# A top-k search on VectorE, with the last round of half the units read from a copy that GpSimd makes

## The chip, the cores and the metric

The kernel runs on one core of a Trainium2 chip. Its engines each work off their own queue in order: TensorE (PE in the profile, PEld for its weight loads), VectorE (DVE), ScalarE (ACT), GpSimd (POOL), and SyncE (SP), which only starts DMAs. They wait for each other through semaphores. The metric is the device time of one execution in microseconds (us); lower is better.

## The reference

Input x is 16 x 512 x 256 in float32. Three blocks follow one another, each added to x after a layernorm: half of an FFN, an attention, and half of the same FFN again.

```
x = x + 0.5 * ffn(layernorm(x))
x = x + attn(layernorm(x))
x = x + 0.5 * ffn(layernorm(x))
```

The attention has 16 heads of 16 columns and keeps, in each row of scores, only those at or above the 31st largest (U = int(5 * log(512)) = 31):

```
scores = einsum('bhqd,bhkd->bhqk', Q, K) / sqrt(D)
thresh = top_k(scores, U)[0][..., -1:]
scores = where(scores < thresh, -inf, scores)
attn = softmax(scores); context = attn @ V; out = context @ Wo.T + bo
```

The FFN routes each row over 16 experts (a gate with a fallback to the two best), mixes q, k and v of the experts by the weights, does causal attention over 512 rows, and mixes again through o_proj.

## The kernel before

The rows are cut into 64 tiles of 128. Three streams run together, each some tiles behind the one before: FFN job b (the first FFN), the attention, and FFN job a (the second). The order is written out by hand: a batch is a window of 64 slots (SPAN), and emit() walks the slots for each engine. The table AT and the constants above it (SC, EV, TOP, OUTS, GAP, TR, ...) say in which slot each step stands. An engine does the slots strictly in order, so a step at slot 7 waits behind everything that its engine has at slots up to 6. Batches 2 to 13 are a hardware loop (Fori), the others are written out.

A unit is one head of one tile: 128 rows by 512 scores. There are 1024; a slot is one unit, four units are a quad, two are a pair. For each quad:
- TensorE makes four score banks at slot 2 (L482), and ScalarE copies them into the ring S of 16 units at slot 3 (L709).
- VectorE searches two pairs, at slots 4 and 6 (TOP, L804 to L818). A search has 7 passes: MAX8 finds the 8 largest of each row and puts them into M8, MATCH_REPLACE writes a copy W in which these 8 are replaced by -3e38, and so on; 4 MAX8 and 3 MATCH_REPLACE. The two units of a pair alternate. The 31st largest is column TH = 30 of M8.
- ScalarE makes OUT = relu(threshold - S) at slot 7 (L720), which is above zero only where a score falls out, and the gap S = max - S at slot 9 (L724).
- TensorE transposes both into a bank, OUT times 2^80 (STEEP), at slot 16 (TR, L516 and L518); ScalarE takes exp (L715); TensorE multiplies by V (L542).

Between these stand the FFN's steps. On GpSimd they are HS (L913, hidden rows times gate weights, for which TensorE waits at L497), mixT (L931), the gate (L887 to L895) and many 1-wide ones for the norms, nmry (L942) among them. On VectorE they are small: v_a and v_b (L789), the replacement for the fallback (L793), a row maximum (L797) and a reciprocal (L784), at the end of a slot, behind a search. held() (L243) is a wait that also raises a counter of its engine. Some names share a buffer group in the profile: M is M8 (in the small jobs, mr is the pair to be replaced), L491 to L500 is the expert product.

Of the kernel before, what the change touches and what calls it, by code (L numbers as in the profile page):

```python
# [120 lines left out]

def build(nc, x, wqk, bqk, wv, bv, wo, bo, sim, gates, wf, wof, out):
    with ExitStack() as ctx:
# [225 lines left out]
        def _(pe):  # L349
# [151 lines left out]
            def slot(w, j):  # L501
# [6 lines left out]
                if at := due(w, j, TR, 4, QUADS * NB):  # L508
                    n, c = at
                    pe.wait_ge(s_ev, w.count(SPAN, 4 * (c + 4)) if w.lo != w.hi else min(4 * (n + 4), UNITS * NB))  # L510
                    for h in range(HG):
                        pe.wait_ge(s_gap, w.count(SPAN, 4 * c + h + 1))
                        r = (4 * c + h) % RING
                        for k in range(TPB):
# [3 lines left out]
                            mm = nc.tensor.matmul(pST[h][:, keys], OUT[:, r, keys], steep[:], start=False, stop=True)  # L518
# [234 lines left out]
        def _(dve):  # L753
# [46 lines left out]
            def slot(w, j):  # L800
# [3 lines left out]
                if at := due(w, j, TOP, 2, PAIRS * NB):  # L804
                    n, c = at
                    src = [S[:, (2 * c + i) % RING, :] for i in range(2)]
                    for k in range(PASSES):
                        for i in range(2):
                            m = M8[:, (2 * c + i) % RING, k // 2 * 8:k // 2 * 8 + 8]
                            if k == 0:  # L810
                                held(dve, s_ev, w.count(SPAN, 2 * c + i + 1))
                            else:
                                held(dve, s_tk, w.count(PAIRS * 2 * PASSES, c * 2 * PASSES + 2 * k + i - 1))
                            if k % 2 == 0:
                                nc.vector.max(m, src[i]).then_inc(s_tk, 1)  # L815
                            else:
                                nc.vector.match_replace(W[:, i, :], m, src[i], -BIG).then_inc(s_tk, 1)  # L817
# [174 lines left out]
```

## Time and profile before

| | |
|---|---|
| timed runs | 4924.1, 4924.43, 4927.03 us; median 4924.43 |
| the profiled execution | 4928.28 us, of which the span is 4925.7 |
| mean granted TensorE clock | 0.916 of full speed |
| busy: VectorE, TensorE, ScalarE, GpSimd | 4551.0, 4153.2, 3405.1, 2370.9 us |
| MAX8, 512 wide | 4096 of them, 0.68 us each |
| MATCH_REPLACE, 512 wide | 3072 of them, 0.68 us each |

Busy time is the time in which at least one instruction of an engine was running; two that overlap count once, so the mean duration of an instruction is longer than its share of the busy time. In a timeline, rows of the same line that follow each other are merged (x2 is two instructions, and the time is that of both). "[1.47 <-DVE M L815]" is idle time ahead of the row and what ended it.

### The profile page before, as it was taken

To read this page: it belongs to the slowest core of one execution; us is meant where nothing else is said; L and a number is where in the kernel's file an instruction comes from. 1 tells how busy PE (TensorE), PEld (TensorE's weight loads), DVE (VectorE), ACT (ScalarE), POOL (GpSimd) and SP (SyncE) were. 2 spreads that over 40 slices of the span, in tenths; PEclk is the share of its full clock that TensorE was granted. 3 is DMA by queue.
4 is the path that set the end of the run, shared out by engine and by line. 5 is a ranking of instruction groups with operands and counts; after the bars stand their busy time and mean duration, and the time that the engine had idled before them with its cause. 6 is when DMAs were issued, how large, how long until landed. Compare 5 with 4: busy or idle time off the path is not lost.

```text
span 4925.7 us, 117907 instructions
## 1 busy us (share of the span) xinstructions
PE 4153.2 (84%) x33100; PEld 3438.4 (70%) x33100; DVE 4551.0 (92%) x10838; ACT 3405.1 (69%) x8261; POOL 2370.9 (48%) x3534
## 2 busy tenths in 40 slices
PE   5767889888988898898889889888998988887767
PEld 4555777777777777777777777777777776765556
DVE  0199999999999999999999999999999999999980
ACT  2366777777777777777777777777777777776652
POOL 4523454545554455555455454545555455532224
PEclk8888999999999999999999999999999999998888
DMA  3110111111111111111111111111111111110011
GB/s 83 53 27 27 44 53 48 55 44 52 49 52 48 46 55 46 52 49 53 45 48 53 46 53 48 55 44 51 53 47 52 46 55 46 51 38 27 18 28 49
DMA packets 244153, 232.77 MB, mean 47 GB/s; under 512 B 27123, under 2 KB 176628, under 8 KB 243316
## 3 DMA queue, kind: packets, MB, share of 16 engines
q1 hardware_dynamic: 243444, 224.49, 16.0%
q8 instruction: 302, 4.95, 0.4%
q14 instruction: 407, 3.33, 0.2%
HBM read 214.98 MB, written 9.44 MB: 46 GB/s over the span
## 4 chain that ended last, share of the span: by engine, by line
issue 55%; DVE 25%; PE 12%; DVEq 4%; POOL 2%; ACT 2%; SPq 0%; DMA 0%; POOLq 0%; ACTq 0%
DVE M L815 15%; DVE W L817 8%; PE pQ L497 5%; DVEq L241 4%; POOL HS L913 1%; PE pST L516 1%; PE pST L482 1%; DVEq L245 1%; PE pFa L442 0%; PE pFb L466 0%; PE pFa L446 0%; PE pST L518 0%; DVE mxr_b L797 0%; ACT S L709 0%; DVE mxr_a L797 0%
## 5 line engine op out<-in xcount | busy, mean ns | idle before, releaser
L497 PE MATMUL pQ<-wf_sb,HS 128*128 128x192 f32 x8192 | 1611.4, 355 | 513.6 <-POOL HS L913 511.8
L815 DVE MAX8 M<-W 128x8 f32<-128x512 f32 x3072 | 1962.8, 681 | 0.0
L497 PEld LDWEIGHTS pQ<-wf_sb,HS 128*128 128x128 f32 x8192 | 1493.8, 210 | 573.5 <-POOL HS L913 505.0
L817 DVE MATCH_REPLACE8 W<-M,W 128x512 f32<-128x512 f32 x2048 | 1369.3, 677 | 0.0
L720 ACT ACTIVATE OUT<-S,M 128x512 bf16<-128x512 f32 x1024 | 747.1, 730 | 399.7 <-DVE M L815 395.3
L516 PE MATMUL pST<-ident,S 128*128 128x128 f32 x4096 | 744.2, 282 | 12.4 <-ACT S L709 12.4
L724 ACT ACTIVATE S<-S,M 128x512 f32<-128x512 f32 x1024 | 735.4, 718 | 0.0
L518 PE MATMUL pST<-steep,OUT 128*128 128x128 bf16 x4096 | 728.5, 221 | 0.0
L817 DVE MATCH_REPLACE8 W<-M,S 128x512 f32<-128x512 f32 x1024 | 684.6, 676 | 0.0
L815 DVE MAX8 M<-S 128x8 f32<-128x512 f32 x1024 | 651.7, 678 | 24.1 <-issue 23.3
L709 ACT COPY S<-pST 128x512 f32<-128x512 f32 x1024 | 524.0, 597 | 205.3 <-PE pST L482 205.3
L516 PEld LDWEIGHTS pST<-ident,S 128*128 128x128 f32 x4096 | 585.3, 143 | 70.8 <-ACT S L709 14.4
L913 POOL TENSOR_TENSOR HS<-hT_a,RB 128x1024 f32<-128x1024 f32 x256 | 604.7, 2362 | 43.1 <-issue 28.2
L715 ACT ACTIVATE PTs<-pST 128x512 f32<-128x512 f32 x1024 | 580.3, 602 | 62.9 <-PE pST L518 30.3
L913 POOL TENSOR_TENSOR HS<-hT_b,RB 128x1024 f32<-128x1024 f32 x256 | 606.4, 2369 | 33.3 <-DMA RB<-rows_b 23.7
L518 PEld LDWEIGHTS pST<-steep,OUT 128*128 128x128 bf16 x4096 | 427.9, 104 | 8.7 <-issue 4.3
L542 PEld LDWEIGHTS pO<-PTs,V 128*32 128x32 f32 x8192 | 216.0, 113 | 211.7 <-issue 198.0
L882 POOL COPY mr_a<-v_a 128x2 f32<-128x2 f32 x64 | 11.8, 184 | 662.7 <-DVE v_a L789 662.7
L482 PE MATMUL pST<-KT,QT 32*128 32x512 f32 x2048 | 303.6, 663 | 9.1 <-ACT PTs L715 9.1
L542 PE MATMUL pO<-PTs,V 128*32 128x128 f32 x8192 | 287.9, 283 | 8.8 <-ACT ctxr L736 5.8
L882 POOL COPY mr_b<-v_b 128x2 f32<-128x2 f32 x64 | 11.8, 184 | 533.0 <-DVE v_b L789 533.0
L878 POOL TENSOR_TENSOR L_a<-Lr_a,sig 128x16 f32<-128x16 f32 x64 | 14.3, 223 | 422.3 <-ACT Lr_a L636 422.3
(219 smaller groups left out, 5654.2 us busy)
## 6 DMA issues: line engine op xcount, KB each, us to landing
RB<-rows_b SPq DMA_DIRECT2D x384, 256.0 KB, 3.3
RB<-rows_a SPq DMA_DIRECT2D x384, 256.0 KB, 3.3
x_b<-in_x SPq DMA_DIRECT2D x64, 128.0 KB, 2.9
out_y<-y SPq DMA_DIRECT2D x64, 128.0 KB, 1.7
wf_sb<-in_wf SPq DMA_DIRECT2D x4, 768.0 KB, 7.0
rows_b<-rwT_b SPq DMA_DIRECT2D x64, 8.0 KB, 1.3
wof_sb<-in_wof SPq DMA_DIRECT2D x1, 1024.0 KB, 7.2
rows_a<-rwT_a SPq DMA_DIRECT2D x64, 8.0 KB, 1.4
```

The source lines that it names most:

```text
L482: nc.tensor.matmul(pST[h][:], QT[r:r + 32, g // 2, g % 2, m * P:(m + 1) * P], KT[r:r + 32, g // 2, :], start=True, stop=True).then_inc(s_s ...
L497: mm = nc.tensor.matmul(pQ[:, 0:QKV], HS[:, k % 2, e, i, :], wf_sb[:, i, at:at + QKV], start=k + e + i == 0, stop=(k, e, i) == (3, 3, 1))
L516: nc.tensor.matmul(pST[h][:, keys], S[:, r, keys], ident[:], is_transpose=True, start=True, stop=False)
L518: mm = nc.tensor.matmul(pST[h][:, keys], OUT[:, r, keys], steep[:], start=False, stop=True)
L542: mm = nc.tensor.matmul(pO[32 * h:32 * h + 32, 0:P], V[:, k, HG * g + h, :], PTs[:, h, k * P:(k + 1) * P], start=k == 0, stop=k == TPB - 1)
L709: nc.scalar.copy(S[:, (4 * c + h) % RING, :], pST[h][:]).then_inc(s_ev, 1)
L715: nc.scalar.activation(PTs[:, h, :], pST[h][:], ACT.Exp, scale=-HD ** -0.5).then_inc(s_pe, 1)
L720: nc.scalar.activation(OUT[:, r, :], S[:, r, :], ACT.Relu, bias=M8[:, r, TH:TH + 1], scale=-1.0)
L724: nc.scalar.activation(S[:, r, :], S[:, r, :], ACT.Identity, bias=M8[:, r, 0:1], scale=-1.0).then_inc(s_gap, 1)
L815: nc.vector.max(m, src[i]).then_inc(s_tk, 1)
L817: nc.vector.match_replace(W[:, i, :], m, src[i], -BIG).then_inc(s_tk, 1)
L913: nc.gpsimd.tensor_tensor(HS[:, k % 2, :, :, :], J.hT[:, c % 2, :].rearrange("p (k t) -> p k t", k=KC).unsqueeze(1).broadcast_to([P, 4, KC ...
```

## The change

Of each four units, the second and the fourth (LIGHT = (1, 3)) are dealt with in another way. VectorE does the first five passes as before: three MAX8 with two MATCH_REPLACE, which give the 24 largest. The 24th largest is M8[:, 23] (FOUND = 24). Then:
- GpSimd, slot 6 or 8: LM = (S >= the 24th) x -2^100 in bfloat16, and XL = S + LM. What has been found is now very low.
- VectorE, the same slot, behind the next pair's search: MAX8 on XL gives the 25th to 32nd.
- ScalarE, one slot later: the sum of LM / 2^100, which is minus the number of scores at or above the 24th (more than 24 if there are ties).
- GpSimd, two slots behind LM: pos = 31 + that sum, pick = (iota == pos), picked = pick x M8[:, 23:31].
- ScalarE, three slots behind: the sum of picked goes to M8[:, 30] as the threshold.

OUT moves from slot 7 to slot 9 and the gap from 9 to 10. OUT has 8 places in its ring in place of 16, and so a wait for the transposes of two quads back. The searches of a pair are issued by a list ORDER, as the second unit has two passes fewer.

```diff
+LIGHT = (1, 3,)
+FOUND = 8 * (ROUNDS - 1)
+ORDER = [(p, i, k) for p in range(2) for k in range(PASSES) for i in range(2) if k < PASSES - 2 or 2 * p + i not in LIGHT]
+LOWER = 2.0 ** 100
+HALF = RING // 2
-SC, EV, TOP, OUTS, GAP, TR, PTE, PV, CT, CTT, CTX = 2, 3, 4, 7, 9, 16, 17, 18, 19, 20, 21
+SC, EV, TOP, OUTS, GAP, TR, PTE, PV, CT, CTT, CTX = 2, 3, 4, 9, 10, 16, 17, 18, 19, 20, 21
+LOW, LTOP, LCNT, LPICK, LTH = 6, 6, 7, 8, 9
...
+def passed(w, c, k):
+    p, i = c % 4 // 2, c % 2
+    return w.count(QUADS * len(ORDER), c // 4 * len(ORDER) + ORDER.index((p, i, k)) + 1)
+
+def light(w, j, slot):
+    for k, u in enumerate(LIGHT):
+        if at := due(w, j, slot + u // 2 * 2, 4, QUADS * NB):
+            n, c = at
+            return n * len(LIGHT) + k, c * len(LIGHT) + k, 4 * c + u
+    return None
...
-        OUT = sb("OUT", P, RING, T, dtype=BF16)
+        OUT = sb("OUT", P, HALF, T, dtype=BF16)
+        LM = sb("LM", P, 2, T, dtype=BF16)
+        XL = sb("XL", P, 2, T)
...
(ScalarE)
+                if at := light(w, j, LCNT):
+                    n, c, u = at
+                    wait(act, s_lpos, n - 1)
+                    held(act, s_low, n + 1)
+                    nc.scalar.activation(spare[:], LM[:, c % 2, :], ACT.Identity, scale=1.0 / LOWER,
+                                         accum_out=cnt[:, c % 2, :]).then_inc(s_lcnt, 1)
+                if at := light(w, j, LTH):
+                    n, c, u = at
+                    held(act, s_lval, n + 1)
+                    nc.scalar.activation(spare8[:], picked[:, c % 2, :], ACT.Identity,
+                                         accum_out=M8[:, u % RING, TH:TH + 1]).then_inc(s_lth, 1)
                 if at := due(w, j, OUTS, 1, UNITS * NB):
...
+                    if c % 4 in LIGHT:
+                        held(act, s_lth, w.count(QUADS * len(LIGHT), c // 4 * len(LIGHT) + LIGHT.index(c % 4) + 1))
+                    else:
+                        held(act, s_tk, passed(w, c, PASSES - 1))
+                    wait(act, s_pt, w.count(SPAN, c // 4 * 4 - 4))
+                    nc.scalar.activation(OUT[:, r % HALF, :], S[:, r, :], ACT.Relu, bias=M8[:, r, TH:TH + 1], scale=-1.0)
...
(VectorE)
+                    for p, i, k in ORDER:
+                        u = 2 * c + i
+                        if p != c % 2:
+                            continue
...
+                if at := light(w, j, LTOP):
+                    n, c, u = at
+                    held(dve, s_lx, n + 1)
+                    nc.vector.max(M8[:, u % RING, FOUND:FOUND + 8], XL[:, c % 2, :]).then_inc(s_ltop, 1)
...
(GpSimd)
+                if at := light(w, j, LOW):
+                    n, c, u = at
+                    r = u % RING
+                    wait(pool, s_lcnt, n - 1)
+                    held(pool, s_tk, passed(w, u, PASSES - 3))
+                    nc.gpsimd.tensor_scalar(LM[:, c % 2, :], S[:, r, :], M8[:, r, FOUND - 1:FOUND], -LOWER, ALU.is_ge, ALU.mult
+                                            ).then_inc(s_low, 1)
+                    wait(pool, s_ltop, n - 1)
+                    pool.wait_ge(s_low, n + 1)
+                    nc.gpsimd.tensor_tensor(XL[:, c % 2, :], S[:, r, :], LM[:, c % 2, :], ALU.add).then_inc(s_lx, 1)
+                if at := light(w, j, LPICK):
+                    n, c, u = at
+                    r = u % RING
+                    held(pool, s_lcnt, n + 1)
+                    nc.gpsimd.tensor_scalar(pos[:], cnt[:, c % 2, :], float(TH + 1), 0.0, ALU.add, ALU.max).then_inc(s_lpos, 1)
+                    wait(pool, s_lval, n)
+                    held(pool, s_lpos, n + 1)
+                    nc.gpsimd.tensor_scalar(pick[:], iota[:], pos[:], None, ALU.is_equal).then_inc(s_lpick, 1)
+                    pool.wait_ge(s_lpick, n + 1)
+                    wait(pool, s_lth, n - 1)
+                    pool.wait_ge(s_ltop, n + 1)
+                    nc.gpsimd.tensor_tensor(picked[:, c % 2, :], pick[:], M8[:, r, FOUND - 1:FOUND + 7], ALU.mult
+                                            ).then_inc(s_lval, 1)
                 for n in "ab":
                     ffn(jobs[n], w, j)
```

VectorE's queue before, one pair from its first MAX8 to the next pair's. M<-S is a MAX8 on the scores, W<-M,S a MATCH_REPLACE from them, W the copy that is searched next:

```order
L815 MAX M<-S 128x8 [waits s_ev] x2
L817 MATCH_REPLACE W<-M,S 128x512 [waits s_tk] x2
L815 MAX M<-W 128x8 [waits s_tk] x2
L817 MATCH_REPLACE W<-M,W 128x512 [waits s_tk] x2
L815 MAX M<-W 128x8 [waits s_tk] x2
L817 MATCH_REPLACE W<-M,W 128x512 [waits s_tk] x2
L815 MAX M<-W 128x8 [waits s_tk] x2
L815 MAX M<-S 128x8 [waits s_ev] x2
```

VectorE's queue after, one pair and the MAX8 on XL that follows it:

```order
L866 MAX M<-S 128x8 [waits s_ev] x2
L868 MATCH_REPLACE W<-M,S 128x512 [waits s_tk] x2
L866 MAX M<-W 128x8 [waits s_tk] x2
L868 MATCH_REPLACE W<-M,W 128x512 [waits s_tk] x2
L866 MAX M<-W 128x8 [waits s_tk] x2
L868 MATCH_REPLACE W<-M,W 128x512 [waits s_tk]
L866 MAX M<-W 128x8 [waits s_tk]
L873 MAX M<-XL 128x8 [waits s_lx]
L838 MAX v_b<-L_b 128x8 [waits shift_b]
```

The third MATCH_REPLACE and the last MAX8 are single now, both of the pair's first unit, and the MAX8 on XL is the previous pair's light unit.

GpSimd's queue before, from the gate's last step to two HS further on (REGISTER_ALU and ISA are steps of its sequencer for waits):

```order
L895 TENSOR_TENSOR mk_a<-fb_a,pos_a 128x16 [waits gate_a]
L924 TENSOR_TENSOR rrs_b<-rs_b,minus_one 128x1 [waits sc_exp_b]
L877 REGISTER_ALU
L878 TENSOR_TENSOR L_b<-Lr_b,sig 128x16 [waits read_b]
L911 ISA
L241 REGISTER_ALU [waits s_rb0]
L913 TENSOR_TENSOR HS<-hT_b,RB 128x1024 [waits s_qk]
L899 TENSOR_TENSOR em_a<-eg_a,mk_a 128x16 [waits gate_exp_a]
L882 COPY mr_b<-v_b 128x2 [waits top_b]
L241 REGISTER_ALU [waits s_rb1]
L913 TENSOR_TENSOR HS<-hT_b,RB 128x1024 [waits s_qk]
```

GpSimd's queue after, at an even slot with mr_a and HS:

```order
L1007 TENSOR_SCALAR LM<-S,M 128x512 [waits s_tk]
L1010 REGISTER_ALU [waits s_ltop]
L1011 TENSOR_TENSOR XL<-S,LM 128x512 [waits s_low]
L1016 TENSOR_SCALAR pos<-cnt 128x1 [waits s_lcnt]
L1019 TENSOR_SCALAR pick<-iota,pos 128x8 [waits s_lval,s_lpos]
L1023 TENSOR_TENSOR picked<-pick,M 128x8 [waits s_ltop,s_lth,s_lpick]
L275 REGISTER_ALU
L939 COPY mr_a<-v_a 128x2 [waits top_a]
L968 ISA
L275 REGISTER_ALU [waits s_rb0]
L970 TENSOR_TENSOR HS<-hT_a,RB 128x1024 [waits s_qk]
```

In every even slot five instructions now stand ahead of what GpSimd had there; pos, pick and picked are those of the light unit one pair back.

## Rows read from the trace of the kernel before

**Rows 1.** The page: busy time, share of the span and instructions by engine.
```profile
PE 4153.2 (84%) x33100; PEld 3438.4 (70%) x33100; DVE 4551.0 (92%) x10838; ACT 3405.1 (69%) x8261; POOL 2370.9 (48%) x3534
```
**Rows 2.** A stretch: its length, busy PE, PEld, DVE, ACT, POOL, clock, DMA.
```profile
600.00:4200.00 3600.00, 3176.41 (x26043) 2650.50 (x26042) 3576.73 (x8514) 2668.96 (x6494) 1865.09 (x2773) 0.94 0.17 50
```
**Rows 3.** Waits from 900 to 4200 us: total, times, longest.
```profile
POOL mr_a L882 <- DVE v_a L789: 475.2, 46, 11.0
...
DVE M L815 <- issue: 23.3, 11, 2.3
```
**Rows 4.** Timeline of VectorE, pairs of searches: start, length, instruction.
```profile
2410.18 1.27 DVE L815 MAX8 M<-S 128x8 f32<-128x512 f32 x2
2411.36 0.08 DVE L817 MATCH_VALUE_LOAD W<-M,S 128x8 f32 x1
...
2412.68 1.28 DVE L815 MAX8 M<-W 128x8 f32<-128x512 f32 x2
...
2418.88 1.27 DVE L815 MAX8 M<-S 128x8 f32<-128x512 f32 x2
...
2436.56 1.28 DVE L815 MAX8 M<-S 128x8 f32<-128x512 f32 x2
```
**Rows 5.** Timeline of VectorE: program start, first search, end of the last.
```profile
2.81 0.16 DVE L758 TENSOR_SCALAR gate_row<-gate_row 1x16 f32<-1x16 f32 x1
3.01 0.24 DVE L760 RECIPROCAL gate_row<-gate_row 1x16 f32<-1x16 f32 x1
...
226.97 1.29 DVE L815 MAX8 M<-S 128x8 f32<-128x512 f32 x2 [0.84 <-ACT S L709]
...
4788.80 0.16 DVE L789 MAX8 v_a<-L_a 128x8 f32<-128x16 f32 x1
```
**Rows 6.** Groups of instructions on GpSimd: busy, mean ns, idle before and its end.
```profile
L913 POOL TENSOR_TENSOR HS<-hT_b,RB 128x1024 f32<-128x1024 f32 x256 | 606.4, 2369 | 33.3 <-DMA RB<-rows_b 23.7 <-PE pQ L497 9.7
L889 POOL TENSOR_SCALAR pos_a<-L_a 128x16 f32<-128x16 f32 x64 | 17.6, 275 | 0.0
L888 POOL TENSOR_SCALAR na_a<-v_a 128x1 f32<-128x1 f32 x64 | 14.1, 221 | 0.0
L838 POOL TENSOR_SCALAR_AFFINE_SELECT ident<-ident 128x128 f32<-128x128 f32 x1 | 0.3, 293 | 0.0
```
**Rows 7.** Timeline of GpSimd, one HS, and from mr_a on.
```profile
2409.92 2.38 POOL L913 TENSOR_TENSOR HS<-hT_a,RB 128x1024 f32<-128x1024 f32 x1
...
2436.63 0.18 POOL L882 COPY mr_a<-v_a 128x2 f32<-128x2 f32 x1 [10.98 <-DVE v_a L789]
...
2440.34 0.30 POOL L942 TENSOR_SCALAR nmry<-mny,rstdy 128x1 f32<-128x1 f32 x1 [0.21 <-POOL rstdy L847]
...
2444.18 2.36 POOL L913 TENSOR_TENSOR HS<-hT_a,RB 128x1024 f32<-128x1024 f32 x1
```
**Rows 8.** Timeline of ScalarE.
```profile
2402.11 0.71 ACT L720 ACTIVATE OUT<-S,M 128x512 bf16<-128x512 f32 x1
2402.72 0.71 ACT L724 ACTIVATE S<-S,M 128x512 f32<-128x512 f32 x1
...
2419.84 0.21 ACT L586 ACTIVATE eg_b<-em_b 128x16 f32<-128x16 f32 x1
2419.95 0.19 ACT L586 ACTIVATION_READ_ACCUMULATOR eg_b<-em_b 128x1 f32 x1
...
2446.51 2.05 ACT L709 COPY S<-pST 128x512 f32<-128x512 f32 x4 [1.76 <-PE pST L482]
```
**Rows 9.** Timeline of TensorE, twice 16 matmuls on HS.
```profile
2401.53 2.77 PE L497 MATMUL pQ<-wf_sb,HS 128*128 128x192 f32 x16
...
2439.25 4.44 PE L497 MATMUL pQ<-wf_sb,HS 128*128 128x192 f32 x16 [7.69 <-POOL HS L913]
```
**Rows 10.** The stretch in which TensorE starved; the third number from the end is the clock.
```profile
2436.00:2454.00 18.00, 14.75 (x108) 12.97 (x109) 18.00 (x46) 10.43 (x26) 14.69 (x22) 0.82 0.25 66
```

More of the change, by code:

```diff
@@ L163, in build @@
         M8 = sb("M8", P, RING, 8 * ROUNDS)
-        OUT = sb("OUT", P, RING, T, dtype=BF16)
+        OUT = sb("OUT", P, HALF, T, dtype=BF16)
+        LM = sb("LM", P, 2, T, dtype=BF16)
+        XL = sb("XL", P, 2, T)
+        spare = sb("spare", P, T, dtype=BF16)
+        iota = sb("iota", P, 8)
+        cnt = sb("cnt", P, 2, 1)
+        pos = sb("pos", P, 1)
+        pick = sb("pick", P, 8)
+        picked = sb("picked", P, 2, 8)
+        spare8 = sb("spare8", P, 8)
         PTs = sb("PTs", P, HG, T)
@@ L517, in slot @@
                                              start=True, stop=False)
[L518 removed]
+                            mm = nc.tensor.matmul(pST[h][:, keys], OUT[:, r % HALF, keys], steep[:], start=False, stop=True)
                         mm.then_inc(s_pt, 1)
@@ L806, in slot @@
                     src = [S[:, (2 * c + i) % RING, :] for i in range(2)]
[L807 to L817, printed above, removed]
-                                src[i] = W[:, i, :]
+                    for p, i, k in ORDER:
+                        u = 2 * c + i
+                        if p != c % 2:
+                            continue
+                        m = M8[:, u % RING, k // 2 * 8:k // 2 * 8 + 8]
+                        if k == 0:
+                            held(dve, s_ev, w.count(SPAN, u + 1))
+                        else:
+                            held(dve, s_tk, passed(w, u, k - 1))
+                        if k % 2 == 0:
+                            nc.vector.max(m, src[i]).then_inc(s_tk, 1)
+                        else:
+                            nc.vector.match_replace(W[:, i, :], m, src[i], -BIG).then_inc(s_tk, 1)
+                            src[i] = W[:, i, :]
+                if at := light(w, j, LTOP):
+                    n, c, u = at
+                    held(dve, s_lx, n + 1)
+                    nc.vector.max(M8[:, u % RING, FOUND:FOUND + 8], XL[:, c % 2, :]).then_inc(s_ltop, 1)
                 for n in "ab":
@@ L829, in _ @@
             nc.gpsimd.memset(ones[:], 1.0)
+            for k in range(8):
+                nc.gpsimd.memset(iota[:, k:k + 1], float(k))
             nc.gpsimd.memset(minus_half[:], -0.5)
```

4 lines of the change are left out of this document (2 added, 2 removed).

## The prediction

> **What bounds the kernel now.** I read the shares of the engines first. VectorE is busy for 4551 of 4926 us, 92%, TensorE for 84%, ScalarE for 69%, GpSimd for 48% [rows 1]. A mean over the whole span hides the stages, so next the stretches: from 600 to 4200 us VectorE is busy for 3577 of 3600 us, while TensorE has 3176, ScalarE 2669 and GpSimd 1865 [rows 2]. The list of waits of the middle of the span says the same from the other side: VectorE's only wait there is 23 us of "issue" (11 times, once for each turn of the loop), while GpSimd waits 475 us in 46 tiles for the small maximum v_a, which stands behind a search in VectorE's queue [rows 3]. So VectorE's queue sets the pace of the middle, and the others lean on it. Its work is the search: 1024 units in 512 pairs, each pair 4 MAX8 and 3 MATCH_REPLACE for each of two units, and from the first MAX8 of one pair to that of the next it takes 2418.88 - 2410.18 = 8.70 us [rows 4]. The search begins at 226.97 and ends at 4788.80: 4562 us, or 71.3 us for each of the 64 tiles (16 units, 8 pairs each) [rows 5]. The 227 us ahead and 137 us behind are a chain of small steps that the change hardly touches.
>
> **What goes from VectorE.** In half the units, two in each four, the third MATCH_REPLACE goes; the MAX8 behind it stays, but reads XL. A MATCH_REPLACE with its value load takes (2412.68 - 2411.36) / 2 = 0.66 us from start to start [rows 4]. 512 of them: 338 us.
>
> **What VectorE pays back.** Until now two units alternate, so an instruction never needs the result of the one right ahead of it. In the changed order the third MATCH_REPLACE of the first unit and its last MAX8 stand back to back, once in a pair. Two things are then lost. The overlap: two MAX8 have 1.27 us on the page, but the next instruction starts 2411.36 - 2410.18 = 1.18 us after the first, so each overlaps its follower by about 0.09 us [rows 4]. And the wait for an own result: 0.04 us between two VectorE instructions at the start of the program (2.81 + 0.16 to 3.01) [rows 5]; on GpSimd it is 0.21 us where a counter is raised behind the wait (held, as here) [rows 7]. The price is between 0.13 and 0.30 us; I take 0.18, nearer to VectorE's own row: 92 us. Net 338 - 92 = 246 us, or 3.8 us a tile: VectorE alone would need 67.5 us.
>
> **What GpSimd takes on.** For each of the 512 light units: LM (one input, 512 wide), XL (two inputs, 512 wide), and pos, pick, picked (1 to 8 wide). It stands in every even slot ahead of the FFN's instructions, so HS, nmry and mixT come later by all of it. XL: HS is 1024 wide and takes 2.37 us; half of it is 1.18, and as the 0.22 us of a 1-wide instruction is not halved, 1.29 [rows 6]. LM has no row of its size. From below: a one-input instruction of 128 wide took 0.29 us [rows 6], 0.07 above the 1-wide one, so another 384 columns add 0.21: 0.5 us. From above: 16 wide took 0.275 and 1 wide 0.22 [rows 6], which is 3.6 ns a column and makes 512 about 2.0 us. I take 0.9, nearer to the wide row. The small ones, by the 1-wide and 16-wide rows: 0.22 + 0.275 + 0.22 us, and for the three waits on own results some 0.37 together, as only pick's has the 0.21 of held [rows 6, 7]: 1.1 us. In all 3.3 us a light unit, bounds 2.75 and 4.4. GpSimd has 1865 / 3600 x 71.3 = 36.9 us a tile now [rows 2], and about 2.1 us in which it waits for itself (some ten times 0.21, by its row in one norm) [rows 7]: 39.0. With 8 x 3.3 it is 65.4 us, 97% of VectorE's 67.5. This is the number on which the case stands: it binds from 3.56 us a light unit.
>
> On two-input work the trace shows 2.37 us for 1024 columns, 2.3 ns a column [rows 6]. The Trainium skill (GPSIMD Engine Reference, section 3.1, Elementwise) has some 2.6 cycles an element there and calls GpSimd about half as fast as VectorE, which speaks against moving work to it: by its rate XL alone is an estimated 1.1 us, more than the 0.66 that it frees. The trace agrees with the rate. For a one-input body the same section has 1.8 cycles and 769 ns for 512 elements; by that LM is an estimated 0.8 to 1.0 us and GpSimd stays just under VectorE. No run here shows it yet.
>
> **Others.** ScalarE: a 512-wide ACTIVATE starts 0.61 us ahead of the next, an accumulator read starts 0.11 us behind its 16-wide ACTIVATE [rows 8] and, as it overlaps like the others, adds about 0.10: 0.71 us for the count and 0.21 for the threshold. That is 0.92 us a light unit, 7.4 a tile, on 2669 / 3600 x 71.3 = 52.9. That is 60.3 of 67.5 us, hidden but for waits. TensorE gets no new instruction: 62.9 us a tile, at a mean clock of 0.94; 93% of 67.5. Where it had been starved of HS, its clock was 0.82 [rows 10] and 16 matmuls took 4.44 us, in a fed stretch 2.77 [rows 9]. OUT's ring of 8 makes ScalarE wait for the transposes of two quads back, in TensorE's queue one slot earlier than ScalarE's own: I cost it at nothing, as the units are now dealt with 2 slots later, too. The ends: eight small memsets, and the last unit's detour over GpSimd and ScalarE: about 5 us.
>
> **What becomes late next.** GpSimd's work is uneven. From mr_a to the next HS it had 2444.18 - 2436.63 = 7.6 us [rows 7]; with 3.3 that is 10.9 against a pair's 8.2 (8.70 - 0.66 + 0.18). Its mean is 65.4 / 8 = 8.2, so it catches up only in the lighter stretches. VectorE needs XL only after the next pair, some 6 us after it can be ready. But ScalarE's copies of new scores S ended at 2448.5, where VectorE wanted them 2 pairs after 2436.56, at 2454.0: 5.5 us to spare [rows 4, 8]. They stand behind nmry, nm_b and TensorE's HS, all late by 1.3 to 3.3 us, and VectorE comes 1 us earlier. One to four us remain, with three engines at 90 to 97%. I put 1.6 us of new waits a tile into VectorE's queue over the 50 tiles of the middle (3600 / 71.3): 81 us. It is the softest term, between 0 and 5 us a tile.
>
> **Sum**, against the profiled execution's 4928.3: 4928.3 - 338 + 92 + 5 + 81 = 4768. The median of the timed runs lies 3.9 us below the profiled one; so 4764 us.
>
> **The rivals.**
> Clean: nothing waits and the bubble is small: 4928.3 - (338 - 64) + 5 - 3.9 = 4655. For it: VectorE waits for nobody today. Against: three engines above 90%.
> GpSimd sets the pace, under today's: at 3.8 us a light unit it needs 39 + 30.4 + 1.6 = 71.0 us a tile; the middle gains 0.3 x 50 = 15, the 13.5 tiles outside it 3.8 x 13.5 = 51: 4863 us.
> Slower: LM costs what the narrow rows say. At 4.4 us a light unit GpSimd needs 39 + 35.2 + 1.6 = 75.8 us a tile, 4.5 above today's: 4928.3 + 227 - 51 + 5 - 3.9 = 5105. It decides from 3.96 us on, where the middle loses what the ends gain. For it: the one-input rows of 16 wide. Against: the row of 128 wide.
> Round trip: no engine is full, but GpSimd, ScalarE and TensorE hand over in turn (LM, its count, pos, picked, the threshold) and the scores come late: at 5 us a tile 4928.3 + (67.5 + 5 - 71.3) x 50 - 51 + 5 - 3.9 = 4938. The queues have 1 or 2 pairs of room there, which speaks against so much.
> That it doesn't do what it says would be GpSimd slowing VectorE's searches while it works; against this, the two MAX8 at 2410.18 have 1.27 us while HS runs from 2409.92, and those at 226.97, long before the stream is full, 1.29 [rows 4, 5, 7].
>
> **How the numbers follow.** The forecast (VectorE sets the pace, with some waits, 4690 to 4840) gets 0.45; clean 0.08; GpSimd the pace but faster 0.17; the round trip 0.12 (0.04 faster, 0.05 same, 0.03 slower); LM dear, slower, 0.18. A change of 0.2%, 10 us, is what a measurement can tell. Faster 0.74, same 0.05, slower 0.21. The range 4650 to 4990 leaves out about 0.02 below and some 0.12 above; the forecast's own is 4690 to 4840.
>
> **What would show it.** In the profile after: MAX8 on XL 512 times and 512 MATCH_REPLACE fewer; a bubble of 0.1 to 0.3 us behind the third MATCH_REPLACE; LM near 0.9 and XL near 1.28 us; GpSimd busy near 90% in the middle; a tile of about 69 us; VectorE waiting for XL or for S by one to two us a tile. Wrong it is if LM comes near 2 us, if GpSimd's waits for VectorE are gone and VectorE waits 5 us a tile or more, or if MAX8 itself is longer beside LM and XL.

## The result and the profile after

| | before | after |
|---|---|---|
| timed runs | 4924.1 to 4927.03, median 4924.81 us | 5180.95 to 5188.01, median 5183.55 us |
| the profiled execution, its span | 4928.28, 4925.7 us | 5184.85, 5182.4 us |
| mean granted TensorE clock | 0.916 | 0.923 |

Over four runs each, the ratio is 1.0526, with a 95% interval of 1.0507 to 1.0544: slower by 259 us, where 4764 us was forecast. The time also lies outside the range of 4650 to 4990.

The page, busy time by engine, to be held against [rows 1]:

```profile
PE 4253.6 (82%) x33100; PEld 3498.0 (67%) x33100; DVE 4285.2 (83%) x9814; ACT 3808.1 (73%) x10309; POOL 4373.3 (84%) x6102
```

VectorE lost 266 us of work (4551.0 to 4285.2), as meant, and the program is longer all the same. Now no engine is full. The same stretch as in [rows 2]: its length, busy PE, PEld, DVE, ACT, POOL, clock, DMA.

```profile
600.00:4200.00 3600.00, 3046.35 (x24259) 2522.14 (x24258) 3136.96 (x7173) 2779.34 (x7541) 3198.08 (x4453) 0.95 0.17 46
```

VectorE idles 463 of 3600 us where it idled 23. GpSimd, with 3198, is the busiest engine, at 89%. The waits from 900 to 4200 us of the kernel after (total, times, longest), against [rows 3]:

```profile
PE pQ L531 <- POOL HS L970: 417.3, 156, 5.6
DVE mxr_a L846 <- ACT Sr_a L686: 263.8, 43, 7.7
ACT x_a L659 <- PE pFa L420: 219.6, 43, 7.0
...
DVE M L873 <- POOL XL L1011: 53.3, 57, 1.5
...
POOL LM L1007 <- DVE M L866: 26.9, 36, 2.9
DVE v_b L838 <- POOL L_b L935: 26.5, 43, 0.6
```

GpSimd's wait of 475.2 us for v_a is gone. VectorE has three new ones: for Sr_a once in each of 43 tiles, 6.1 us each time, for XL, and for L_b. ScalarE's wait for x_a and TensorE's for HS, both longer than before, suggest that the trail of the largest one leads over both back to GpSimd. The same two in the kernel before:

```profile
PE pQ L497 <- POOL HS L913: 323.6, 79, 7.7
...
ACT x_a L625 <- PE pFa L386: 68.3, 46, 1.8
```

TensorE waited for HS before, too, without holding up VectorE; so these sums alone prove nothing, and the trail is followed in time further down.

GpSimd's groups of instructions in the kernel after, against [rows 6]: busy, mean ns, idle before and its end.

```profile
L1007 POOL TENSOR_SCALAR LM<-S,M 128x512 bf16<-128x512 f32 x512 | 1033.4, 2018 | 180.4 <-issue 106.0 <-DVE M L866 33.8
L970 POOL TENSOR_TENSOR HS<-hT_a,RB 128x1024 f32<-128x1024 f32 x256 | 605.5, 2365 | 14.7 <-DMA RB<-rows_a 9.2 <-PE pQ L531 5.1
...
L1011 POOL TENSOR_TENSOR XL<-S,LM 128x512 f32<-128x512 f32 x512 | 593.1, 1158 | 51.9 <-POOL LM L1007 14.8 <-ACT spare L754 0.6
L1019 POOL TENSOR_SCALAR pick<-iota,pos 128x8 f32<-128x8 f32 x512 | 165.3, 323 | 98.1 <-issue 97.9 <-POOL pos L1016 0.2
...
L1016 POOL TENSOR_SCALAR pos<-cnt 128x1 f32<-128x1 f32 x512 | 120.2, 235 | 46.8 <-ACT spare L754 2.1
L1023 POOL TENSOR_TENSOR picked<-pick,M 128x8 f32<-128x8 f32 x512 | 104.8, 205 | 44.5 <-POOL pick L1019 2.8
```

LM takes 2018 ns, where 900 was assumed. HS is what it was (for hT_b 2369 ns before and 2361 now, by the page), so it has not become dearer beside the new work. The same in time, one light unit in GpSimd's queue of the kernel after:

```profile
2442.01 2.01 POOL L1007 TENSOR_SCALAR LM<-S,M 128x512 bf16<-128x512 f32 x1
2444.10 1.15 POOL L1011 TENSOR_TENSOR XL<-S,LM 128x512 f32<-128x512 f32 x1
2445.34 0.23 POOL L1016 TENSOR_SCALAR pos<-cnt 128x1 f32<-128x1 f32 x1
2445.76 0.31 POOL L1019 TENSOR_SCALAR pick<-iota,pos 128x8 f32<-128x8 f32 x1 [0.19 <-issue]
2446.16 0.20 POOL L1023 TENSOR_TENSOR picked<-pick,M 128x8 f32<-128x8 f32 x1
2446.30 0.18 POOL L939 COPY mr_b<-v_b 128x2 f32<-128x2 f32 x1
```

From 2442.01 to 2446.30 it is 4.29 us a light unit (three others near it take 4.34 to 4.36), against 3.3 forecast. Seen from VectorE (kernel after, timeline of the same tile):

```profile
2407.33 0.67 DVE L868 MATCH_REPLACE8 W<-M,W 128x512 f32<-128x512 f32 x1
2407.93 1.27 DVE L866 MAX8 M<-W 128x8 f32<-128x512 f32 x2
...
2409.18 0.67 DVE L868 MATCH_REPLACE8 W<-M,W 128x512 f32<-128x512 f32 x1
2410.00 0.70 DVE L866 MAX8 M<-W 128x8 f32<-128x512 f32 x1
2410.61 0.68 DVE L873 MAX8 M<-XL 128x8 f32<-128x512 f32 x1
2411.20 0.16 DVE L838 MAX8 v_a<-L_a 128x8 f32<-128x16 f32 x1
...
2439.56 0.18 DVE L838 MAX8 v_b<-L_b 128x8 f32<-128x16 f32 x1 [0.61 <-POOL L_b L935]
...
2447.49 0.68 DVE L873 MAX8 M<-XL 128x8 f32<-128x512 f32 x1
2454.51 0.42 DVE L846 TENSOR_REDUCE mxr_a<-Sr_a 128x1 f32<-128x256 f32 x1 [6.34 <-ACT Sr_a L686]
```

The bubble lies between the rows at 2409.18 and 2410.00: 0.82 us from the third MATCH_REPLACE to the MAX8 that reads its result and waits for its semaphore. In the first two rows, where the MAX8 reads the result of an earlier instruction, it is 0.60, so the bubble is 0.22 us. The last row is the wait that matters: VectorE stands still for 6.34 us for a small FFN step, with all further searches behind it. What it waited for, first on TensorE, then on ScalarE:

```profile
2441.78 4.18 PE L531 MATMUL pQ<-wf_sb,HS 128*128 128x192 f32 x16 [3.64 <-POOL HS L970]
2445.76 1.44 PE L418 MATMUL pFa<-wo_sb,ctxT 128*128 128x256 f32 x4
```
```profile
2448.49 0.38 ACT L659 ACTIVATE x_a<-pFa 128x256 f32<-128x256 f32 x1 [5.73 <-PE pFa L420]
...
2449.87 2.05 ACT L743 COPY S<-pST 128x512 f32<-128x512 f32 x4 [0.54 <-PE pST L516]
...
2453.96 0.41 ACT L686 COPY Sr_a<-pFa 128x256 f32<-128x256 f32 x1
```

TensorE waited 3.64 us for HS, ran its 16 matmuls in 4.18 us, near the 4.44 of the starved stretch in [rows 9], and only then did the output projection behind them in its queue, for which ScalarE had been idle for 5.73 us. So the delay of HS on GpSimd is handed over through two more queues, and reaches VectorE as a wait for ScalarE.

### The profile page after: what moved, and what is told of

It reads as the page before. It is cut to its first block and busy times, and to the rows that moved or that the text cites. A ratio compares the mean times of both kernels' runs of the same rounds, so it can differ in the third digit from the quotient of the medians.

```text
span 5182.4 us, 125169 instructions
## 1 busy us (share of the span) xinstructions
PE 4253.6 (82%) x33100; PEld 3498.0 (67%) x33100; DVE 4285.2 (83%) x9814; ACT 3808.1 (73%) x10309; POOL 4373.3 (84%) x6102
## 5 line engine op out<-in xcount | busy, mean ns | idle before, releaser
L531 PE MATMUL pQ<-wf_sb,HS 128*128 128x192 f32 x8192 | 1668.7, 364 | 663.1 <-POOL HS L970 662.4
L531 PEld LDWEIGHTS pQ<-wf_sb,HS 128*128 128x128 f32 x8192 | 1536.0, 215 | 749.9 <-POOL HS L970 633.1
L866 DVE MAX8 M<-W 128x8 f32<-128x512 f32 x2560 | 1662.4, 682 | 75.7 <-DVE W L868 1.5
L1007 POOL TENSOR_SCALAR LM<-S,M 128x512 bf16<-128x512 f32 x512 | 1033.4, 2018 | 180.4 <-issue 106.0
L868 DVE MATCH_REPLACE8 W<-M,W 128x512 f32<-128x512 f32 x1536 | 1028.8, 674 | 0.0
L1011 POOL TENSOR_TENSOR XL<-S,LM 128x512 f32<-128x512 f32 x512 | 593.1, 1158 | 51.9 <-POOL LM L1007 14.8
L970 POOL TENSOR_TENSOR HS<-hT_b,RB 128x1024 f32<-128x1024 f32 x256 | 604.4, 2361 | 32.0 <-DMA RB<-rows_b 25.4
L873 DVE MAX8 M<-XL 128x8 f32<-128x512 f32 x512 | 347.4, 679 | 66.8 <-POOL XL L1011 66.7
L846 DVE TENSOR_REDUCE mxr_a<-Sr_a 128x1 f32<-128x128 f32 (+1 forms) x64 | 31.1, 486 | 430.3 <-ACT Sr_a L686 430.3
L754 ACT ACTIVATE spare<-LM 128x512 bf16<-128x512 bf16 x512 | 331.1, 647 | 0.0
```

The source lines that it names most:

```text
L531: mm = nc.tensor.matmul(pQ[:, 0:QKV], HS[:, k % 2, e, i, :], wf_sb[:, i, at:at + QKV], start=k + e + i == 0, stop=(k, e, i) == (3, 3, 1))
L970: nc.gpsimd.tensor_tensor(HS[:, k % 2, :, :, :], J.hT[:, c % 2, :].rearrange("p (k t) -> p k t", k=KC).unsqueeze(1).broadcast_to([P, 4, KC ...
L1007: nc.gpsimd.tensor_scalar(LM[:, c % 2, :], S[:, r, :], M8[:, r, FOUND - 1:FOUND], -LOWER, ALU.is_ge, ALU.mult).then_inc(s_low, 1)
L1011: nc.gpsimd.tensor_tensor(XL[:, c % 2, :], S[:, r, :], LM[:, c % 2, :], ALU.add).then_inc(s_lx, 1)
```

## The experiments

**What LM costs by itself.** A program of 80 us with nothing of the kernel's work: fourteen forms of instruction on GpSimd, four times over, and 48 MAX8 on VectorE beside the last turns.

```
for k in range(4):
    nc.gpsimd.tensor_scalar(O["two_ops_ptr_bf16"][:], S[:], t, -LOWER, ALU.is_ge, ALU.mult)   # LM as it is
    ...
    nc.gpsimd.tensor_scalar(O["mult_add_imm"][:], S[:], 0.5, 1.0, ALU.mult, ALU.add)
    nc.gpsimd.tensor_tensor(O["add_f32"][:], S[:], S[:], ALU.add)
    nc.gpsimd.tensor_copy(O["copy_f32"][:], S[:])
    ...
```

> A small program of its own that does none of the reference's work: GpSimd runs fourteen instruction forms on 128 rows, four times over, the last two times with 48 MAX8 of 512 columns running on VectorE. It asks why LM takes 2.02 us where 0.9 was assumed. If the tensor_scalar path as such costs 3.6 ns a column (the slope of the 16-wide rows of before), every tensor_scalar of 512 columns takes 1.8 to 2.1 us, with one operation or two, immediate or pointer, float32 or bfloat16 out, and 256 and 128 columns take about 1.1 and 0.7 us. If the second operation costs, the one-operation forms take about 1.2 us; if the pointer costs, the immediate forms do; if the conversion to bfloat16 costs, the float32 form is shorter; if the compare costs, mult alone is about 1.0 us. tensor_tensor of 512 columns: 1.16 us as in the changed kernel. Sharing of a port with VectorE would show as longer times in the last two turns, or as MAX8 above 0.68 us; I expect neither.

Groups by form, busy and mean ns (min_ptr_f is a multiplication by a pointer's value):

```profile
L66 DVE MAX8 top<-S 128x8 f32<-128x512 f32 x48 | 28.6, 682 | 39.7 <-POOL narrow_ptr L57 39.7
L44 POOL TENSOR_SCALAR two_ops_ptr_bf<-S,thr 128x512 bf16<-128x512 f32 x4 | 8.0, 1997 | 0.5 <-POOL thr L39 0.2
...
L47 POOL TENSOR_SCALAR two_ops_imm_f<-S 128x512 f32<-128x512 f32 x4 | 7.7, 1927 | 0.3
...
L48 POOL TENSOR_SCALAR one_mult_imm_f<-S 128x512 f32<-128x512 f32 x4 | 6.0, 1497 | 0.3
L49 POOL TENSOR_SCALAR one_ge_imm_f<-S 128x512 f32<-128x512 f32 x4 | 6.0, 1492 | 0.0
L56 POOL TENSOR_SCALAR half_ptr<-S,thr 128x256 f32<-128x256 f32 x4 | 4.6, 1158 | 0.3
...
L57 POOL TENSOR_SCALAR narrow_ptr<-S,thr 128x128 f32<-128x128 f32 x4 | 2.9, 717 | 0.3
...
L51 POOL TENSOR_SCALAR mult_add_imm<-S 128x512 f32<-128x512 f32 x4 | 2.5, 621 | 0.0
```

LM's price is the instruction's own: 1997 ns here, alone, against 2018 in the kernel. Neither the bfloat16 output nor the pointer makes it (both taken away: 1927). Nor is it the comparison: alone it is 1492, a multiplication alone 1497, a copy 611 (not shown), and only mult with add is as cheap, 621. Why that one is cheap the run does not show. The three widths of LM's form, 717, 1158 and 1997, lie on 3.3 to 3.4 ns a column; the 16-wide rows of [rows 6] had said 3.6. The MAX8 beside all this takes 682 ns, as ever.

**Moved slots and smaller ring, without light units.**

```diff
-LIGHT = (1, 3,)
+LIGHT = ()
```

> The changed kernel with LIGHT empty: all units are searched with 4 MAX8 and 3 MATCH_REPLACE by VectorE, but OUT stands at slot 9, the gap at 10, and OUT's ring has 8 places. Theory (GpSimd's queue is full): these moves cost nothing, 4915 to 4935 us, VectorE's tile stays 71.3 us. Rival (the later slots and the short ring make ScalarE wait for the transposes and hold up the scores): a good part of the 258 us is here already, 4980 us or more.

4928.53 us over ten runs, against 4925.47 on that chip: a ratio of 1.0005 (0.9995 to 1.0014). OUT and the gap two slots later, and a ring of 8, cost nothing that can be told.

**VectorE's part alone.** GpSimd's and ScalarE's new instructions are left out, and the last MAX8 reads S itself, so the threshold isn't the reference's.

```diff
...
-                    held(dve, s_lx, n + 1)
-                    nc.vector.max(M8[:, u % RING, FOUND:FOUND + 8], XL[:, c % 2, :]).then_inc(s_ltop, 1)
+                    nc.vector.max(M8[:, u % RING, FOUND:FOUND + 8], S[:, u % RING, :]).then_inc(s_ltop, 1)
...
```

> VectorE's part alone: two of four units lose their third MATCH_REPLACE, the last MAX8 reads S in place of XL, and GpSimd and ScalarE get none of the new instructions; the threshold of these units is not the reference's. Theory: VectorE sets the pace, each pair saves 0.66 us and loses the 0.235 us that the changed trace shows ahead of the dependent MAX8 (0.83 from start to start in place of 0.595), 0.425 x 512 = 218 us: 4700 to 4730 us. Rival (VectorE's new order itself costs, by the bubble and by what stands behind it): 4850 us or more. Rival (TensorE or ScalarE can't go faster than now): it stays above 4800 with VectorE waiting for S.

4727.66 us, ratio 0.959 (0.9574 to 0.9606). The stretch from 600 to 4200 us:

```profile
600.00:4200.00 3600.00, 3261.61 (x27202) 2743.70 (x27201) 3503.18 (x8060) 2775.18 (x6772) 1939.91 (x2878) 0.95 0.19 52
```

So 198 us is what the change takes from VectorE, net of the bubbles (against 4925.47 on that chip), and 456 us is what the new work of GpSimd and ScalarE gives back on top (5183.55 - 4727.66).

**LM at the price that was assumed.** LM only 192 columns wide; the others stay zero, so part of the mask is not computed.

```diff
-nc.gpsimd.tensor_scalar(LM[:, c % 2, :], S[:, r, :], M8[:, r, FOUND - 1:FOUND], -LOWER, ALU.is_ge, ALU.mult
+nc.gpsimd.tensor_scalar(LM[:, c % 2, 0:192], S[:, r, 0:192], M8[:, r, FOUND - 1:FOUND], -LOWER, ALU.is_ge, ALU.mult
```

> The changed kernel with LM made for 192 of the 512 columns only (the rest of LM stays zero, so the threshold is not the reference's); everything else, all waits and hand-overs, as in the change. By 3.6 ns a column LM takes about 0.9 us, which is what the prediction took for the whole of it. Theory (GpSimd's queue): its tile falls from 75.3 by 8 x 1.1 to 66.5 us, below VectorE's 67.9, and VectorE sets the pace again with one to two us of waits a tile: 4710 to 4800 us. Rival (round trip of hand-overs between GpSimd, ScalarE and VectorE, not the load): the hop is 1.1 us shorter but stays, one turn in two slots, so less than a quarter of the loss goes: above 5050 us.

4855.57 us, ratio 0.9853 (0.9837 to 0.987), above the 4710 to 4800 that were expected. GpSimd's LM, and two of VectorE's and GpSimd's waits from 900 to 4200 us:

```profile
L1009 POOL TENSOR_SCALAR LM<-S,M 128x192 bf16<-128x192 f32 x512 | 487.2, 952 | 369.4 <-issue 221.7 <-DVE M L866 117.3
```
```profile
POOL LM L1009 <- DVE M L866: 106.3, 105, 1.5
DVE mxr_a L846 <- ACT Sr_a L686: 105.2, 46, 3.3
```

With LM at 0.95 us the change is a gain of 1.5%: LM's price alone decides the sign. But it is not the forecast's 4764. Against the kernel of VectorE alone it loses 128 us, 2.0 us a tile in all, where 1.6 over 50 tiles was put.

**The same load elsewhere in GpSimd's queue.** LM 192 wide as before, and behind picked an instruction of 320 columns whose result nobody reads; the rest of LM is not computed.

```diff
...
+                    held(pool, s_load, n)
+                    nc.gpsimd.tensor_scalar(load[:, 0:320], S[:, r, 192:512], 0.5, -LOWER, ALU.is_ge, ALU.mult).then_inc(s_load, 1)
```

> As the kernel with LM 192 columns wide, and a compare-and-multiply of the other 320 columns into a buffer that nobody reads stands behind picked in GpSimd's queue: the load of the changed kernel, but no hand-over waits for it. Theory (GpSimd's queue is full): the loss is back, 5150 to 5300 us (one more instruction's start, about 0.3 us, in each light unit makes 8 x 0.3 x 64 = 150 us on top possible). Rival (the time from LM to XL to the MAX8 on XL, a matter of latency): it stays near 4856 us, under 4900.

5341.04 us, ratio 1.0841 (1.0823 to 1.0859), more than the 5150 to 5300 that were expected. XL is ready 1.07 us sooner after LM's start than in the changed kernel, and yet the program is 157 us longer: what counts here is how long GpSimd is occupied, not how long XL takes to come. The added instruction had 1.30 us and a wait in front of it, more than the 1.07 that LM gave up.

**Half as many light units.**

```diff
-LIGHT = (1, 3,)
+LIGHT = (3,)
```

> The changed kernel with LIGHT = (3,), one light unit in four. Theory: GpSimd needs 39 + 4 x 4.7 = 57.8 us a tile, VectorE 71.3 - 4 x 0.425 = 69.6, so VectorE sets the pace and the saving is 0.425 x 256 = 109 us: 4815 to 4870 us with waits up to 0.8 us a tile. Rival (each light unit costs by its round trip): half of the change's loss, about 5050 us.

4824.33 us, ratio 0.9792 (0.9776 to 0.9809). From 600 to 4200 us:

```profile
600.00:4200.00 3600.00, 3211.73 (x26621) 2657.82 (x26614) 3540.93 (x8293) 2893.90 (x7465) 2698.61 (x3860) 0.98 0.19 51
```

VectorE is the bound again, its only wait from 900 to 4200 us 29.1 us of "issue", and half the dose brings 101 us (against 4925.59 on that chip), half of the 198 of VectorE alone.

**LM 352 wide**, to see whether the time follows LM in a straight line:

```diff
-nc.gpsimd.tensor_scalar(LM[:, c % 2, :], S[:, r, :], M8[:, r, FOUND - 1:FOUND], -LOWER, ALU.is_ge, ALU.mult
+nc.gpsimd.tensor_scalar(LM[:, c % 2, 0:352], S[:, r, 0:352], M8[:, r, FOUND - 1:FOUND], -LOWER, ALU.is_ge, ALU.mult
```

> The changed kernel with LM made for 352 of 512 columns (the rest of LM stays zero), a third point between 512 (5183.5 us) and 192 (4855.6). LM should take 0.95 + 160 x 3.33 ns = 1.49 us, 0.53 less than in the change. Theory (GpSimd's queue sets the pace at this point too): all of it comes back, 0.53 x 512 = 273 us: 4905 to 4925 us, about even with the kernel before. That is the point that the prediction put at 3.96 us a light unit. Rival (the loss lies in steps, as ScalarE and TensorE just miss their slots): well off that line, under 4880 or over 4980 us.

5029.63 us (5009.33 to 5036.37 over four runs), ratio 1.0193 (1.017 to 1.0215), with LM at 1487 ns: a miss. From 2018 to 1487 ns only 154 us came back, and from 1487 to 952 another 174, where each step takes some 273 us of work from GpSimd (0.533 x 512). About 0.6 of what is saved arrives. To see where, I cut the tiles between 1500 and 3900 us at the starts of v_a and mxr_a on VectorE, L_b on GpSimd and x_a on ScalarE, and took means over 30 to 33 tiles (the rows above give one: 2411.20, 2439.20 (L_b, not shown), 2448.49, 2454.51):

| us | v_a to L_b | L_b to x_a | x_a to mxr_a | mxr_a to v_a | tile |
|---|---|---|---|---|---|
| before | 15.4 | 10.9 | 9.3 | 35.9 | 71.5 |
| after, LM 2.02 | 27.3 | 9.0 | 6.1 | 34.5 | 76.9 |
| LM 1.49 | 24.5 | 8.9 | 6.1 | 34.6 | 74.1 |
| LM 0.95 | 22.1 | 8.1 | 6.1 | 34.5 | 70.8 |

From mxr_a to v_a the tile takes the same 34.5 us, whatever LM costs: there VectorE sets the pace, 1.4 us faster than before, and GpSimd catches up and waits for it at an LM (26.9 us in the waits of after, 29.6 with 352 columns, 106.3 with 192). The stretch from v_a to L_b answers with 2.8 and 2.4 us, about five times 0.53; it is GpSimd's. Only three LM stand in it; the others are those ahead of v_a, since GpSimd's last wait, with which it arrives late. From L_b to mxr_a no LM is on the way, only HS, TensorE and ScalarE. By this reading about five of a tile's eight LM count: 5 x 0.53 x 64 = 170 us, near both steps.

In the second step 0.8 us more came between L_b and x_a, and there the traces show TensorE's granted clock. Cut tile by tile, that stretch takes 7.6 us where its granted clock is 1.00, the higher of the two levels (2.4 GHz) all along, 9.0 to 9.3 us where it is 0.81 or 0.82, and 10.4 to 10.6 where it is 0.67 or 0.68. This holds in all three kernels; only the mix differs: 9, 15 and 6 of 30 tiles with LM at 2.02 us, 11, 13 and 7 of 31 at 1.49, and 24, 9 and none of 33 at 0.95. In the kernel before the clock is 1.00 there in all 33 tiles, though the stretch is 10.9 us long, which I did not trace. The tile followed above, where TensorE had stood idle for 3.64 us for HS, is one of those at 0.82 (the third number from the end):

```profile
2439.20:2448.49 9.29, 6.71 (x26) 5.78 (x27) 8.42 (x19) 3.40 (x12) 8.75 (x11) 0.82 0.13 28
```

So part of LM's price comes back through TensorE's clock; what sets the mix was not tested. Two longer stretches, of 18 us from L_b to mxr_a, first with 352, then with 192 columns, show it as well:

```profile
2446.00:2464.00 18.00, 14.87 (x98) 12.02 (x97) 11.29 (x25) 10.57 (x32) 14.18 (x22) 0.81 0.12 31
```
```profile
2422.00:2440.00 18.00, 17.14 (x123) 11.96 (x121) 15.95 (x39) 14.95 (x40) 15.89 (x25) 1.00 0.09 30
```

Which LM count was tested by two kernels; in each of them two of the eight LM of a tile are 192 wide.

**The two behind L_b.** The other columns of those two are not computed.

```diff
...
+                    k = 192 if j % 16 in (10, 12) else T
+                    nc.gpsimd.tensor_scalar(LM[:, c % 2, 0:k], S[:, r, 0:k], M8[:, r, FOUND - 1:FOUND], -LOWER, ALU.is_ge, ALU.mult
```

> The changed kernel with LM only 192 columns wide in two of the eight light units of a tile, those whose LM stands in GpSimd's queue between L_b and nm_a (slots 10 and 12 of each 16); the other columns of those two are not computed. That takes 2 x 1.066 us of GpSimd's work from every tile, 136 us in all. My theory from the starts of L_b, x_a, Sr_a and mxr_a: no LM stands in the chain L_b, HS, TensorE, x_a, Sr_a, mxr_a, and behind it VectorE sets the pace and GpSimd waits for it, so these two are idle time made longer: 0 to 45 us less, 5140 to 5184. The rival, that GpSimd's load counts alike wherever it stands: a quarter of the 328 us that eight narrow ones gave, 82 us less, about 5102.

**The two ahead of L_b.**

```diff
...
+                    k = 192 if j % 16 in (6, 8) else T
+                    nc.gpsimd.tensor_scalar(LM[:, c % 2, 0:k], S[:, r, 0:k], M8[:, r, FOUND - 1:FOUND], -LOWER, ALU.is_ge, ALU.mult
```

> The same with the two narrow ones at slots 6 and 8 of each 16, between mr_a and L_b in GpSimd's queue; the other columns of those two are not computed. My theory: the stretch from v_a to L_b is set by GpSimd alone, so nearly all of the 136 us comes back: 110 to 136 us less, 5048 to 5074. The rival, that load counts alike wherever it stands: 82 us less, about 5102, as in the kernel sent with it.

Behind L_b: 5184.35 us, ratio 1.052 (1.0502 to 1.0537). Ahead of it: 5048.66, ratio 1.0248 (1.0231 to 1.0265). LM's groups and VectorE's largest wait, first behind L_b, then ahead of it:

```profile
L1010 POOL TENSOR_SCALAR LM<-S,M 128x192 bf16<-128x192 f32 x128 | 120.6, 942 | 44.8 <-issue 34.3
```
```profile
DVE mxr_a L846 <- ACT Sr_a L686: 274.6, 43, 7.8
```
```profile
L1010 POOL TENSOR_SCALAR LM<-S,M 128x192 bf16<-128x192 f32 x128 | 121.7, 951 | 23.7 <-DVE M L866 6.9 <-issue 4.5
```
```profile
DVE mxr_a L846 <- ACT Sr_a L686: 248.6, 45, 6.6
```

The same 136 us taken from GpSimd's work give nothing in one place and 135 us in the other. That load counts alike wherever it stands is refuted. The 135 us are not all GpSimd's own, though: cut as above, of the 2.1 us that a tile's two LM gave up ahead of L_b, 1.8 arrive between v_a and L_b (25.5 us); 0.6 more come between L_b and x_a (8.4 us), where TensorE's granted clock is 1.00 in 16 of 31 tiles and 0.81 or 0.82 in the others. Behind L_b the tile stays at 77.1 us.

**The mask by ScalarE.** ScalarE makes LM = relu(2^80 x S - 2^80 x the 24th), XL = S - LM on GpSimd, and the last MAX8 goes to M8[:, 23:31]: the 24th itself stays at its value, so the 31st largest stands at column 30 without a count. pos, pick, picked and both sums on ScalarE go.

```diff
...
+nc.scalar.activation(neg[:, c % 2, :], M8[:, r, FOUND - 1:FOUND], ACT.Copy, scale=-STEEP).then_inc(s_lcnt, 1)
+nc.scalar.activation(LM[:, c % 2, :], S[:, r, :], ACT.Relu, bias=neg[:, c % 2, :], scale=STEEP).then_inc(s_low, 1)
...
-nc.vector.max(M8[:, u % RING, FOUND:FOUND + 8], XL[:, c % 2, :]).then_inc(s_ltop, 1)
+nc.vector.max(M8[:, u % RING, FOUND - 1:FOUND + 7], XL[:, c % 2, :]).then_inc(s_ltop, 1)
```

> The same two units of four, but LM is made by ScalarE as relu(2^80 S - 2^80 t), t being the 24th largest, GpSimd only subtracts it (XL), and the MAX8 on XL, which finds the 24th to 31st, writes the threshold itself into column 30: no count, no pos, pick, picked. (Among exactly equal scores at the 24th place the threshold can be one that stands a place higher than the reference's.) GpSimd: 39 + 8 x 1.25 = 49 us a tile; ScalarE as in the change, some 0.85 us a light unit. Theory: VectorE sets the pace, 4720 to 4770 us, as in the kernel with VectorE's part alone (4728) with small waits. Rival (waits of any hand-over to GpSimd and back cost VectorE, whatever the load): 4850 us or more.

4711.77 us, ratio 0.9569 (0.9553 to 0.9585), a little under the 4720 to 4770 that were expected. From 600 to 4200 us:

```profile
600.00:4200.00 3600.00, 3265.34 (x27283) 2702.97 (x27275) 3513.72 (x8083) 3099.33 (x7640) 2419.13 (x3304) 0.98 0.18 52
```

GpSimd is at 67%, ScalarE at 86%, VectorE full again but for its bubbles, with 24.5 us of waits from 900 to 4200 us: the whole gain of VectorE alone arrives.

**With it, both light units in one pair, and three of four:**

```diff
-LIGHT = (1, 3,)
+LIGHT = (0, 1)
```
```diff
-LIGHT = (1, 3,)
+LIGHT = (0, 1, 3)
```

> As the one before, with LIGHT = (0, 1): both units of a quad's first pair are light, so their passes alternate to the end and no MAX8 stands right behind the MATCH_REPLACE that it needs. Theory: the bubble of 0.235 us is gone, VectorE saves the whole 0.66 us 512 times and needs 66.0 us a tile, 4590 us; TensorE (63 us a tile) and ScalarE (60) are near it, so waits of one or two us a tile: 4610 to 4720 us. Rival (TensorE or ScalarE already sets the pace): no faster than the one before.

> The penalty by ScalarE with LIGHT = (0, 1, 3), three light units in four. VectorE needs 71.3 - 12 x 0.66 + 4 x 0.235 = 64.3 us a tile, GpSimd 39 + 12 x 1.25 = 54, ScalarE 52.9 + 12 x 0.85 = 63.1, TensorE 63 at its present clock. Theory (three engines within 2% of each other, none with room): little or nothing is won over two light units, 4620 to 4720 us, with VectorE waiting for ScalarE some us a tile. Rival (VectorE alone still counts): 4570 to 4600 us.

4686.83 us, ratio 0.9521 (0.9505 to 0.9537), and 4681.92 us, ratio 0.9501 (0.9485 to 0.9516). In one pair the two units alternate to the end, so the bubbles go, 0.22 x 512 = 113 us by the price above; 25 us of it arrive, since VectorE now waits 64.4 us for Sr_a and 12.9 for S from 900 to 4200 us. The stretch from 600 to 4200 us, first with the pair, then with three:

```profile
600.00:4200.00 3600.00, 3278.35 (x27358) 2746.29 (x27357) 3491.80 (x8105) 3131.20 (x7661) 2412.40 (x3303) 0.97 0.18 52
```

```profile
600.00:4200.00 3600.00, 3267.94 (x27296) 2719.26 (x27299) 3363.93 (x7648) 3274.99 (x8057) 2643.34 (x3505) 0.98 0.18 52
```

VectorE has 128 us less work there than with the pair, but ScalarE and TensorE are at 91% each and VectorE waits 126.1 us for Sr_a: what the third light unit saves is given back nearly whole. The 5 us between the two kernels lie within the noise: the intervals of their ratios overlap. Both are about 5% faster than before.

## Why the prediction was wrong

**The step that failed** is the price of LM: "LM has no row of its size ... I take 0.9, nearer to the wide row". It is 2.02 us. The row of 128 wide which I followed is an affine_select [rows 6], another instruction; LM's form, a tensor_scalar with two operations, has 717 ns at that width, not 293. Of the two bounds the upper one, from the 1-wide and 16-wide rows, came within 2%: 3.6 ns a column makes it 2.06 us. That is in part luck. Those rows are comparisons with an immediate and no second operation [rows 6], and the same form at 512 columns is 1.49 us in the first experiment: for itself the slope was 0.6 us too dear, and LM's pointer and second operation filled the gap. The trace of before also had a nearer row, which the prediction did not use, a comparison and a multiplication by a pointer's value, 16 wide:

```profile
L893 POOL TENSOR_SCALAR fb_b<-fb_b,na_b 128x16 f32<-128x16 f32 x64 | 24.0, 375 | 14.4 <-POOL nv_b L891 14.4
```

With 375 ns against 275 for the comparison by an immediate it showed that the second operation, the pointer or both are not free. The Trainium skill (GPSIMD Engine Reference, section 3.1, Elementwise), on which an estimate of 0.8 to 1.0 us rested, gives 769 ns for 512 elements, and it calls this the best case, of a tight loop without branches that depend on the data; the prediction took it for any one-input body. The measurements differ on both sides and decide: the copy and mult with add, 611 and 621 ns, are below that figure, and LM is 2.6 times it.

**What hung on it.** A light unit costs GpSimd 4.29 us in place of 3.3, beyond the 3.56 at which the prediction let it bind and the 3.96 at which the sign turns. XL (1.16 for 1.29) and the small ones (0.76 of work and about 0.3 between, for 1.1) were close. The lower bound of 2.75 us is 2.9 by its own terms (0.5 + 1.29 + 1.1); nothing hung on it.

**The slower rival** had the mechanism and nearly the size. It gave the middle a tile of 75.8 us; by the table it is 76.9, 5.4 over before, or 270 us in 50 tiles. And it let the ends gain 51 us, where the result of 259 leaves them a gain of 11. The middle is 43 us more than its 227 and the ends 40 less gain, which is the 79 us by which 5105 was too low, but for the 5 us that it had for the last detour. But it saw GpSimd as the pace of the whole tile, 39 + 8 x 4.29 = 73.3 us, and GpSimd paces only part of it. The 3.6 us above that are idle time of GpSimd: its waits from 900 to 4200 us put 1.2 us a tile on VectorE and ScalarE (26.9 us for a MAX8, 20.3 for x_a and 4.7 for Lr_a over 43 tiles) and 0.4 on "issue" ahead of LM; the rest is in gaps that I did not trace. What fills VectorE's own gap are waits that are handed over: 6.1 us for Sr_a once a tile, behind HS, 16 matmuls and x_a. That was the "round trip" in part, though through HS, which the light units ahead of it delay, and not through the count and the threshold.

**What VectorE saves** was nearly right. The prediction's own terms without waits are 4928.3 - 338 + 92 + 5 - 3.9 = 4683; the kernel of VectorE alone has 4728. The bubble, 0.22 in place of 0.18 us, is 20 us of the difference. Of the other 25 I can name only that VectorE waits there for its own W by the profile, 12 us from 900 to 4200 us. The kernel with the mask on ScalarE has the same work on VectorE and is 16 us faster still (the intervals of the two ratios just overlap); what makes that was not tested.

**The waits**, "the softest term", were 128 us with LM at the assumed price against 81. So with LM right the forecast would still have been 92 us too low (4855.57), though inside its range.

**Right** were: the moved slots and OUT's ring at nothing, ScalarE's count and threshold (0.65 and 0.22 us, their reads overlapped), and that MAX8 is not slowed by GpSimd's work: 681 ns before, 682 after, 682 beside LM's own form. **What would show it wrong** stood in the last part of the prediction, and of its signs all but a longer MAX8 came: LM near 2 us, GpSimd's waits for v_a gone, VectorE waiting 5 us a tile or more (8.0 without "issue": 343.6 us over 43 tiles).

**The chances** were the second fault. Two rows of the same instruction, a tensor_scalar, spoke for 2.0 us; one row of another instruction and the best case of the Trainium skill spoke for less. That earned the dear LM more than 0.18.
